# A windowed attention: a unit's product of values at one place, its sums in a ring of three banks, a fifth place for exponentials, and counts from a scan

## The reference, cut to what matters

```python
q = proj(Wq, bq); k = proj(Wk, bk); v = proj(Wv, bv)      # 16 heads of 16 channels
energy = jnp.einsum('bhqd,bhkd->bhqk', q, k)
energy = jnp.where(jnp.abs(idx[:, None] - idx[None, :]) > 128, fmin, energy)
att = jax.nn.softmax(energy / jnp.sqrt(256.), axis=-1)
out = jnp.einsum('bhqk,bhkd->bhqd', att, v)
x = x + (out @ Wp.T + bp)
logits = layernorm(x) @ Wg + bg                            # 8 experts
one_hot = jax.nn.one_hot(jnp.argmax(logits, axis=-1), 8)
x = x + sum over experts of one_hot * (gelu(xf @ W1[e]) @ W2[e])
```

## Time and profile before

| | us |
|---|---|
| median of 3 runs | 1569.64 |
| lowest and highest | 1557.91, 1571.14 |
| the profiled execution's own time | 1558.37 |
| its span, first to last instruction | 1556.6 |

### The profile page before, as it was taken

The page is one execution under the profiler, slowest core; times in us unless marked ns, Lnnn a source line. Parts: engine busy times, 40 slices in busy tenths (PEclk is TensorE's granted clock), DMA queues, the critical chain, the costliest instruction groups (busy, mean ns, idle before and its releaser), DMA issues.

```text
span 1556.6 us, 23979 instructions
## 1 busy us (share of the span) xinstructions
PE 1441.7 (93%) x7871; PEld 1049.9 (67%) x7871; DVE 704.2 (45%) x2447; ACT 452.3 (29%) x765; POOL 447.5 (29%) x533
## 2 busy tenths in 40 slices
PE   7999999999999999897889889898998899899998
PEld 4566655567777776455555666566665588799998
DVE  5743347323333333337677777777767112300000
ACT  1211211012111111113546555555544511112121
POOL 1100000143222221503344454444222323334342
PEclk9998999999999999898899999999988899999999
DMA  9300100012111111125334444444432477699996
GB/s 336 106 28 27 41 0 1 11 55 62 61 62 62 62 61 48 41 87 153 113 110 126 150 139 121 124 142 144 122 96 91 136 253 255 253 334 338 340 335 235
DMA packets 89095, 204.82 MB, mean 132 GB/s; under 512 B 11629, under 2 KB 45551, under 8 KB 78992
## 3 DMA queue, kind: packets, MB, share of 16 engines
q1 hardware_dynamic: 72512, 167.99, 32.4%
q0 software_dynamic: 12096, 32.13, 6.9%
q10 hardware_dynamic: 4368, 3.17, 0.7%
HBM read 151.48 MB, written 52.17 MB: 131 GB/s over the span
## 4 chain that ended last, share of the span: by engine, by line
PE 79%; DVE 9%; issue 5%; DMA 3%; ACT 2%; ACTq 1%; SPq 0%; another core or an unknown queue 0%; POOL 0%; DVEq 0%; POOLq 0%
PE psum L723 11%; PE psum L605 9%; PE psum L903 8%; PE psum L913 8%; PE psum L702 6%; PE psum L616 5%; PE psum L794 5%; PE psum L749 4%; PE psum L771 3%; DVE work L1731 2%; DMA qT<-max_T 2%; PE psum L821 2%; PE psum L532 2%; PE psum L850 2%; PE psum L684 2%
## 5 line engine op out<-in xcount | busy, mean ns | idle before, releaser
L1731 DVE CUSTOM_DVE_ANT_0 work<-psum,mask 128x384 bf16<-128x384 f32 (+1 forms) x512 | 233.1, 487 | 122.0 <-PE psum L749 116.6
L1138 ACT ACTIVATE arena<-psum 128x512 f32<-128x512 f32 (+1 forms) x256 | 179.5, 703 | 188.0 <-PE psum L771 163.2
L723 PE MATMUL psum<-arena,work 128*128 x568 | 186.6, 472 | 3.0 <-ACT work L1050 2.4
L749 PE MATMUL psum<-kz,qT 96*128 96x384 f32 (+1 forms) x512 | 172.1, 415 | 9.8 <-DVE small L1731 6.8
L1807 POOL DMA_INDIRECT work<-normed,token_of x71 | 67.3, 948 | 352.4 <-PE psum L684 210.8
L771 PE MATMUL psum<-qT,kz 100*128 100x384 f32 (+1 forms) x512 | 131.0, 337 | 28.0 <-ACT arena L1138 16.7
L605 PE MATMUL psum<-arena 128*128 128x512 f32 x320 | 154.2, 628 | 0.0
L903 PE MATMUL psum<-arena 128*128 128x128 f32 x1248 | 148.7, 278 | 2.8 <-ACT arena L1172 2.8
L903 PEld LDWEIGHTS psum<-arena 128*128 128x128 f32 x1248 | 145.4, 195 | 3.0 <-issue 3.0
L749 PEld LDWEIGHTS psum<-kz,qT 96*128 96x128 f32 x512 | 91.4, 199 | 82.0 <-DVE small L1731 38.0
L913 PE MATMUL psum<-arena 128*128 128x256 f32 x624 | 142.8, 383 | 0.8 <-ACT work L986 0.8
(11 more groups left out here) (222 smaller groups left out, 1968.9 us busy)
## 6 DMA issues: line engine op xcount, KB each, us to landing
arena<-in_w SPq DMA_DIRECT2D x78, 1024.0 KB
strips<-hi SPq DMA_DIRECT2D x64, 256.0 KB
kz<-strips SPq DMA_DIRECT2D x64, 192.0 KB, 4.1
qT<-strips SPq DMA_DIRECT2D x32, 384.0 KB, 4.9
results<-work SPq DMA_DIRECT2D x71, 128.0 KB, 1.7
strips<-lo SPq DMA_DIRECT2D x32, 256.0 KB
normed<-work SPq DMA_DIRECT2D x14, 512.0 KB, 3.0
X<-in_x SPq DMA_DIRECT2D x8, 512.0 KB, 9.7
```

The lines of the kernel that those rows point to most:

```text
L723: m = e.matmul(psum[:, pair[u], 0:INTER], xsT0[:, b % 2, c * P:(c + 1) * P], wu0[:, bass.ds(x, 1), c, u * INTER:(u + 1) * INTER], start=(c ...
L749: m = e.matmul(psum[:, bk, at:at + w], qT[0:ROWS_S, slot, half, i * P:(i + 1) * P], kz[slot][0:ROWS_S, hd, lo_key:hi_key], start=True, sto ...
L1138: e.activation(pT[:, j, 2 * half:2 * half + 2, 0:w], src, ACT.Exp, scale=1.0 / E ** 0.5).then_inc(p_exped, 1)
L1731: e.tensor_tensor_reduce(masked[:, n % 2, 0:w], psum[:, bank_of["scores", u, i, hd], at:at + w], mask[:, P - off:P - off + w], 1.0, MASKED ...
```

## The change

It has five parts.
- `pe_values` makes all 16 products of a unit at one place, step 11 in half 1, and takes its bank from the ring of the other work. ScalarE copies the sum in step 12, as before.
- That ring has banks 5, 6 and 7 from step 2 on (`m_ring`), and 6 and 7 before. The second list's bank is 3 instead of 5.
- `pT` has five places, used in turn by all tiles of all units. `act_exp` waits for the values of the whole unit that had its place before: two units back for tile 0, one unit back for the others.
- The fourth place of `pT` lies where the first layer's weights of the first expert block went. The two places of `w1_now` are swapped, the first load waits for the second scores of unit 29, the second for the values of unit 30.
- `dve_pick` makes, by a scan, sums over the tiles of a batch that begin with the running count, and `pe_ranks` needs two products, three where a list follows. `dve_places` copies the count on.

```diff
-def values_due(step):
-
-    return [(u, 0) for u, _ in unit(step, 10, 1)] + [(u, 1) for u, _ in unit(step, 12, 1)]
...
-        pT = carve(arena, 15616, 4, G, 3 * P)
+        pT_slots = [carve(arena, at, G, 3 * P) for at in (15616, 17152, 18688, 27904, 20224)]
...
-        w1_now = [carve(arena, at, EC, HID) for at in (27904, 23808)]
+        w1_now = [carve(arena, at, EC, HID) for at in (23808, 27904)]
...
-        LIST_BANK, LIST_UNITS = (2, 5), range((LISTED_AT[0] + 2) // 4, (PIECES_AT[0][-1] + 1) // 4 + 1)
-        AGAIN, O_BANK, M_RING = (3, 4), 5, (6, 7)
+        LIST_BANK, LIST_UNITS = (2, 3), range((LISTED_AT[0] + 2) // 4, (PIECES_AT[0][-1] + 1) // 4 + 1)
+        AGAIN = (3, 4)
...
+        def m_ring(s):
+
+            return (5, 6, 7) if s > LATER_END else (6, 7)
+
+        def pT(u, j):
+            return pT_slots[(u * TPB + j) % 5]
...
-        def pe_values(e, u, j):
+        def pe_values(e, u, ring):
+
             b, g = divmod(u, NG)
...
+            bk = next_of(ring)
+            fill(e, ("values", u), bk)
+            for j in range(TPB):
+                lo, hi = window(j)
+                e.wait_ge(v_made, TPB * b + j + 1)
+                e.wait_ge(p_masked, u * TPB + j + 1)
+                for hh in range(G):
+                    m = e.matmul(psum[32 * hh:32 * hh + 32, bk, lo:hi], v32[:, b % 2, j, G * g + hh, :],
+                                 pT(u, j)[:, hh, 0:hi - lo], start=(j == 0), stop=(j == TPB - 1), skip_group_check=True)
+            m.then_inc(bank_full[bk], 1)
...
-            for d in range(1, TPB):
-                m = e.matmul(psum[:, bk, d * w:n], ones[:, :], flat[:, 0:n - d * w], start=False, stop=False,
+            e.matmul(psum[:, bk, 0:n], before[:, :], chosen[:, :, 1:], start=True, stop=False, skip_group_check=True)
+            m = e.matmul(psum[:, bk, 0:n], ones[:, :], sums[:, :, 0:TPB], start=False, stop=True, skip_group_check=True)
+            if b in (EARLY_B - 1, B - 1):
+                m = e.matmul(psum[:, bk, n:n + NX], ones[:, :], sums[:, :, TPB], start=False, stop=True,
                              skip_group_check=True)
-            e.wait_ge(so_far_made, b + 1)
-            for t in range(TPB):
-                m = e.matmul(psum[:, bk, t * w:(t + 1) * w], ones[:, :], so_far, start=False, stop=True,
-                             skip_group_check=True)
...
-                        for u, i in values_due(s):
-                            pe_values(e, u, 2 * i)
-                            pe_values(e, u, 2 * i + 1)
+                            pe_maxima(e, u, ring)
                     else:
+                        for u, _ in unit(s, 11, 1):
+                            pe_values(e, u, ring)
...
-            if half == 0 and u > 0:
-                if j < TPB - 1:
-                    e.wait_ge(pT_read, (u - 1) * (TPB - 1) + j + 1)
-                else:
-                    e.wait_ge(*done["values", u - 1])
+            n = u * TPB + j
+            if half == 0 and n >= 5:
+                e.wait_ge(*done["values", (n - 5) // TPB])
...
-            e.tensor_tensor(hot1, cand1, wide(pick), ALU.is_equal).then_inc(picked, 1)
+            yield from dve_link(e, e.tensor_tensor(hot1, cand1, wide(pick), ALU.is_equal))
+            e.wait_ge(so_far_made, b + 2)
+            e.tensor_tensor_scan(sums.rearrange("p x t -> p (x t)"), restart1, chosen.rearrange("p x t -> p (x t)"), 0.0, ALU.mult, ALU.add).then_inc(picked, 1)
...
+            if b < B - 1:
+                e.tensor_copy(chosen[:, :, 0], sums[:, :, TPB]).then_inc(so_far_made, 1)
...
-            if b < B - 1:
-                yield from dve_link(e, e.tensor_reduce(in_batch, hot1.rearrange("p t x -> p x t"), AX.X, ALU.add))
-                e.tensor_tensor(so_far, so_far, in_batch, ALU.add).then_inc(so_far_made, 1)
-                e.wait_ge(so_far_made, b + 2)
...
+            if k == 0:
+                e.wait_ge(*done["again", NU - 3, TPB - 1, G - 1])
             if k == 1:
-                e.wait_ge(*done["again", NU - 3, TPB - 1, G - 1])
+                e.wait_ge(*done["values", NU - 2])
```

More of the change, by code:

```diff
@@ L784, in pe_maxima, with pe_out_rows @@
             m.then_inc(bank_full[bk], 1)
-        def pe_values(e, u, j):
+        def pe_values(e, u, ring):
             b, g = divmod(u, NG)
-            lo, hi = window(j)
-            if j == 0:
-                fill(e, ("values", u), O_BANK)
-            e.wait_ge(v_made, TPB * b + j + 1)
-            e.wait_ge(p_masked, u * TPB + j + 1)
-            for hh in range(G):
-                m = e.matmul(psum[32 * hh:32 * hh + 32, O_BANK, lo:hi], v32[:, b % 2, j, G * g + hh, :],
-                             pT[:, j, hh, 0:hi - lo], start=(j == 0), stop=(j == TPB - 1), skip_group_check=True)
-            if j < TPB - 1:
-                m.then_inc(pT_read, 1)
-            else:
-                m.then_inc(bank_full[O_BANK], 1)
-        def pe_out_rows(e, u):
-            bk = next_of(M_RING)
+            bk = next_of(ring)
+            fill(e, ("values", u), bk)
[7 more added lines that the diff above has]
+            m.then_inc(bank_full[bk], 1)
+        def pe_out_rows(e, u, ring):
+            bk = next_of(ring)
             fill(e, ("o", u), bk)
@@ L807, in pe_out_rows, with pe_qk @@
             m.then_inc(bank_full[bk], 1)
-        def pe_qk(e, b, c, i, k):
+        def pe_qk(e, b, c, i, k, ring):
             xs = NORM[2, b] % 2
@@ L823, in pe_qk, with pe_v @@
                 m.then_inc(bank_full[bk], 1)
-        def pe_v(e, b, t):
+        def pe_v(e, b, t, ring):
             xs = NORM[2, b] % 2
-            bk = next_of(M_RING)
+            bk = next_of(ring)
             fill(e, ("v", b, t), bk)
@@ L832, in pe_v, with pe_project @@
             m.then_inc(bank_full[bk], 1)
-        def pe_project(e, b, c):
-            bk = next_of(M_RING)
+        def pe_project(e, b, c, ring):
+            bk = next_of(ring)
             fill(e, ("project", b, c), bk)
@@ L840, in pe_project, with pe_residual @@
             m.then_inc(bank_full[bk], 1)
-        def pe_residual(e, b, half, t):
+        def pe_residual(e, b, half, t, ring):
             if t == 0:
-                fill(e, ("residual", b, half), next_of(M_RING))
+                fill(e, ("residual", b, half), next_of(ring))
                 e.wait_ge(oT2_made, 2 * (b + 1))
@@ L905, in pe_up1, with pe_down1 @@
                 m.then_inc(bank_full[u], 1)
-        def pe_down1(e, k):
-            bk = next_of(M_RING)
+        def pe_down1(e, k, ring):
+            bk = next_of(ring)
             fill(e, ("down1", k), bk)
@@ L918, in pe_attention @@
             for s in range(FIRST_STEP, LAST_STEP):
+                ring = m_ring(s)
                 for half in range(2):
@@ L961, in pe_attention @@
                         for k in blocks_at(s, DOWN_AT):
-                            pe_down1(e, k)
+                            pe_down1(e, k, ring)
         @block.tensor
@@ L1082, in act_attention @@
                     act_place_maxima(e, u)
-                for u, i in values_due(s):
-                    if i == 1:
-                        if u > 0:
-                            e.wait_ge(*done["o", u - 1])
-                        e.wait_ge(*done["values", u])
-                        e.activation(oT, psum[:, O_BANK, :], ACT.Copy).then_inc(oT_made, 1)
+                for u, _ in unit(s, 12, 1):
+                    if u > 0:
+                        e.wait_ge(*done["o", u - 1])
+                    e.wait_ge(*done["values", u])
+                    e.activation(oT, psum[:, bank_of["values", u], :], ACT.Copy).then_inc(oT_made, 1)
                 for u, j in unit(s, 7, 4):
@@ L1533, in dve_list @@
             if i == 1:
-                left = in_batch
+                left = left_now
                 yield from dve_link(e, e.tensor_tensor(left, n_blocks, taken, ALU.subtract))
```

77 lines of the change are left out of this document (36 added, 41 removed).

## The result

The changed kernel is slower. Over 19 runs of each its median is 1581.2 us against 1562.0 us, a ratio of 1.0106 between the means (1.0123 between the medians), with a 95% interval of 1.0078 to 1.0133. The profiled execution has a span of 1579.5 us against 1556.6 us: 22.9 us more. I had forecast 0.9% faster, 1555 us. That number was laid on a median of three runs, 7.6 us above the median of all 19, so what follows compares differences: -14.5 us forecast, +16.5 us measured by the ratio.

A forecast was written before the change was run, and what follows sets the result against it. The prediction took TensorE to set the end nearly everywhere. Its terms, +3 + 4 - 8 - 12 - 4 + 1.5 + 1 = -14.5 us, laid on a median of 1569.64 us, gave 1555 us, range 1534 to 1577.

The forecast's parts named there:

- The floor in step 2: Step 2, half 0 of a unit: the exponential keeps second products 1.3 us apart, so emptying it saves 0.7 us, not 1.21.
- the forecast of 1.5 us: Step 0, half 0 of a unit: without values, second products stand some 1.5 us apart instead of 3.06, saving 1.5 us.
- The DMA wait: Step 11 of each batch, TensorE waiting for the maxima: 0.5 us lost in each of 8 batches, +4 us.
- The clock: TensorE's granted clock: falls behind bank waits and the fifth batch's long ranks go away, 2 to 3 us each, -4 us.
- My first rival: Clock falls in every batch behind the longer step 11 wait: +17 us, so +2 us in all, 1572 us; chance 0.22.
- The move by itself: A unit's values joined in step 3, half 1: +2.3 - 1.5 - 0.7 = +0.1 us a unit, +3 us over 32 units.
- The third bank: Ring of three banks: the wait of `qk` at L821 and smaller ones go, -8 us; the wait of `project` counts 0.
- The scan: Ranks of a batch: two products left, three where a batch lists; 12.3 us saved, taken as -12 us.
- Lost cover: Rival: the 2.3 us block of values starves VectorE, the bound in steps 1 and 2; at 1 us a unit 1587 us; chance 0.13.
- Weights and end of the stage: First expert's weights loaded later but land in time, cost 0; stage end loses cover under ScalarE's table changes, +1.5 us.
- The test that the prediction named: Step 11: a wait for the maxima near 2 us and the granted clock behind it decide between forecast and first rival.
- two signs of being wrong: Second products in step 0 going well under 1.5 us apart, or waits for VectorE appearing in steps 1 and 2.

The follow-up runs named there:

- the filled wait: Kernel after plus two matmuls that nothing reads, ahead of the wait for the maxima in each odd unit; ratio 0.9997 to the kernel before.
- the last kernel: Kernel after with every second unit's values ahead of the long waits for maxima, and ScalarE copying these a half sooner; 0.9837 to the kernel before, median 1537.0 us.
- the two kernels: Kernel after with values in a bank of their own and a ring of two, 1.0198 to the kernel before; and the kernel after itself, 1.0106.

## Why the prediction was wrong, step by step

- **The floor in step 2: wrong, and part of the rest.** I took the time from one second product to the next there as 1.3 us at least, set by the exponential, so that 0.7 us would be saved. It is 0.70 us, and 1.3 us is saved. Kernel after, step 2 and then step 0:

```profile
860.27 0.50 PE L779 MATMUL psum<-qT,kz 100*128 100x256 f32 x2 [0.25 <-ACT arena L1133]
860.62 0.52 PE L757 MATMUL psum<-kz,qT 96*128 96x384 f32 x2
860.97 0.40 PE L779 MATMUL psum<-qT,kz 100*128 100x256 f32 x2
```

```profile
757.18 0.51 PE L779 MATMUL psum<-qT,kz 100*128 100x384 f32 x2
...
758.68 0.62 PE L779 MATMUL psum<-qT,kz 100*128 100x384 f32 x2 [0.31 <-ACT arena L1133]
```

  In step 0 the forecast of 1.5 us holds exactly: 384 columns fill both banks in each half. With 256 columns two heads share a bank and each half has one of its own, so the second half waits for no exponential of the first. The code says so (`AGAIN[half]`), and I used one floor for both. It is not the root of all: at 860.28 and 935.49 us the wait grew by 3.0 us, of which 0.6 us is this error.
- **The DMA wait, the term that was mis-sized.** I booked +4 us, 0.5 us at step 11 of 8 batches. From 700 to 1260 us it is +33 us, at two steps a batch. I reasoned from the one wait that the trace showed. I should have asked of each unit how much work lies between the issue and the need: 6.5 us in step 9 to 11, with 7.8 us to land. Nor does 0.5 us follow from my own words, that what step 2 saves becomes wait and part of what step 0 saves: with 0.7 and 1.5 us booked as saved that is 0.7 us at least. At step 11 the wait grew by 2.6 us a batch on the average, 1.6 us of it work that is gone behind the issue and 1.1 us a later landing. The maxima land 9 to 11 us after the strips, before and after, so what the shorter step 0 saves ahead of their issue, 0.7 to 1.0 us, mostly turns into wait. The units that showed no wait had little to spare. At step 3 the first two waits (3.0 and 3.2 us) have the 4.6 us of work that step 11 has; the four behind them (1.0 to 2.1 us) have 6.4 us, beside a landing of 7.4 to 8.5 us.
- **The clock: the sign was wrong.** I booked -4 us for falls that go away. They do, and new ones come in every batch. My first rival had the mechanism, the place and the condition. Its price, +17 us, was about right or somewhat low: the clock costs 17 us by the filled wait, some 20 us by the two windows (busy time +11 us, with about 10 us less of ranks) and 25 us by the last kernel. What it left out is most of the waits (+15 us of idle time net), and it saw falls at step 11 alone. It gave 1572 us, 2 us above its own base, where 16.5 us were measured. The Trainium skill, TensorE: Matmul & The Clock Gate, section on HAM oscillation, says that waits for DMA in each tile cost the clock anew each time; by that rule alone the rival would have been the forecast, and the traces agree with it, 1.00 against 0.68 in the window of step 11, and 1.00 again where the wait was filled.
- **The move by itself, +3 us: not seen.** It can't be separated from the waits that it causes; together they are 3.0%, some 47 us.
- **The third bank: right.** -8 us booked; 14 us between the two kernels, with -0.9%, give or take 10. L821's wait went, and that of `project` went to `residual` as said (5.6 us at L857 for 6.5).
- **The scan: right.** -12 us booked; 16.5 us alone, with 12 us inside its interval, and 4 of its gain already into the DMA wait there. In the full change only 0.4%, some 6 us, is left of it: ranks stand ahead of step 11, and what is saved ahead of a late transfer is waited for.
- **Lost cover, the slower rival: no.** Waits of L757 for VectorE are 10.3 us against 6.8, those of L779 for ScalarE 14.8 against 12.1 up to the experts. Small beside 33, and not tested by a kernel of its own.
- **Weights and end of the stage.** The stretch from the first expert block on is 3 us shorter. Waits for gathered rows are 8.2 us there in two (5.5 at 1323.95 us), against one of 2.6 us before; no kernel tells whether it comes from the order of the weights, and I leave it open.

The test that the prediction named, the clock behind step 11, did decide: for the rival. The two signs of being wrong that it named did not: step 0 has its 1.5 us, and the waits for VectorE grew by 3.5 us only.

## What to carry to other kernels

For each transfer that comes back into the chain, write down the work that lies between its issue and its use, beside its time to land, also where no wait shows yet, and count from the large transfers ahead of it where these decide when it lands; whoever shortens that stretch pays in waits and, on TensorE, in clock. A block of work that is free to move belongs in front of the longest wait for something that doesn't come sooner: here the change, scan included, is 1.1% slower with a unit's 16 products of values behind that wait and 1.6% faster with those of every second unit ahead of it (and their copy half a step sooner). Moving the issue to an earlier place costs the issuing engine its queue time, 1.2 us here, where none of its own work runs beside it.

## What the runs showed of the hardware

- Two pieces of 8 KB land within 2.6 us with the strips, keys and queries held back. With 768 KB of strips issued 2 to 3 us ahead of them by another engine, and the keys within 1 us of them, they take 6.5 to 8.0 us at step 11 before and 8.0 to 9.0 us after; counted from the strips it is 9.2 to 11.0 us in both.
- Two issues of DMA by ScalarE hold up its next activation by 1.3 us ([1.33 <-issue]).
- Work that nothing reads, 1.9 us in each of 16 waits, made the kernel 1.1% faster (1.0106 to 0.9997): TensorE's granted clock stayed at 1.00 in a window of step 11 where it had been 0.68.
- The same products in another order took TensorE 468.4 us of busy time at a mean clock of 0.88 and 443.8 us at 0.95.
- The lower level also came behind or at waits of 1.0 us (899.92 and 968.85 us), while waits of 1.3 us in the kernel before had none.
